# Rounding of the feed-forward rows on GpSimd, tiles written out, the last tile in quarters, and small steps with two tensors

## The reference

```python
x = x + xattn(layernorm(x), ctx)              # 16 heads, 1024 keys per batch
x = x + ffn(layernorm(x))                     # hidden width 2048

def bit_linear(x, w, b):
    gamma_x = clip(max(abs(x), axis=-1), 1e-5)
    x_dq = clip(round(x * 127 / gamma_x), -128, 127) * gamma_x / 127
    gamma_w = clip(mean(abs(w)), 1e-5)
    w_dq = clip(round(w / gamma_w), -1, 1) * gamma_w
    return x_dq @ w_dq.T + b

def ffn(x):
    return bit_linear(silu(bit_linear(x, gate_w, gate_b)) * bit_linear(x, val_w, val_b), out_w, out_b)
```

## Time and profile before

| what | us |
|---|---|
| three runs | 858.44, 861.84, 864.04 |
| median | 861.84 |
| profiled execution, span from first to last instruction (the page gives no other time of it) | 861.5 |
| TensorE busy | 757.3 (88%) |
| VectorE busy | 766.2 (89%) |
| ScalarE busy | 573.6 (67%) |
| GpSimd busy | 577.6 (67%) |

### The profile page before, as it was taken

One profiled execution on the slowest core, in us unless ns is written; L12 is line 12 of the kernel. 1 busy time (PEld: TensorE's weight loads), 2 busy tenths in 40 slices (PEclk: granted clock), 3 DMA queues, 4 the chain that ended last, 5 costly groups with the idle time before them and its releaser, 6 DMA issues.

```text
span 861.5 us, 12578 instructions
## 1 busy us (share of the span) xinstructions
PE 757.3 (88%) x3268; PEld 487.1 (57%) x3268; DVE 766.2 (89%) x1026; ACT 573.6 (67%) x838; POOL 577.6 (67%) x581
## 2 busy tenths in 40 slices
PE   3678998989999999999999999999999675868996
PEld 3555565756666666666566656665666442424543
DVE  5799899989998999899989999999999767797895
ACT  2477677767766867687667766776777576774332
POOL 5769674867486757766776668576848474867462
PEclk9889999999999999999999999999999797889999
DMA  9216867776768576858676766677668999400000
GB/s 330 79 49 115 169 130 140 138 167 134 151 114 170 117 161 132 170 111 167 118 160 134 152 128 138 149 137 150 125 146 213 241 227 275 164 0 25 13 24 37
DMA packets 294405, 118.50 MB, mean 138 GB/s; under 512 B 271856, under 2 KB 278000, under 8 KB 294128
## 3 DMA queue, kind: packets, MB, share of 16 engines
q1 hardware_dynamic: 293568, 116.68, 62.0%
q10 hardware_dynamic: 816, 1.57, 0.5%
HBM read 49.02 MB, written 2.10 MB: 59 GB/s over the span
## 4 chain that ended last, share of the span: by engine, by line
PE 35%; POOL 20%; DVE 18%; issue 11%; DMA 7%; SPq 5%; ACT 3%; POOLq 1%; DVEq 0%; ACTq 0%
PE banks L1419 22%; POOL rot_cos L1055 5%; PE scores L1720 5%; DMA load<-in_pack 4%; POOL rot_lo L1063 4%; SPq L943 4%; PE scores L1507 3%; PE banks L1735 3%; DVE neg_max L1323 3%; POOL rot_hi L1061 2%; DVE rows L1330 2%; POOL rot_sin L1046 2%; DVE rot_cos L1295 2%; DVE cv_lo L1288 1%; POOL wq_lo L388 1%
## 5 line engine op out<-in xcount | busy, mean ns | idle before, releaser
L1185 ACT ACTIVATE scores<-scores,neg_max 128x1024 f32<-128x1024 f32 x128 | 139.2, 1087 | 56.1 <-DVE neg_max L1323 54.6
L1330 DVE SCALAR_TENSOR_TENSOR rows<-scores,rows 128x1024 f16<-128x1024 f32 x128 | 154.9, 1220 | 13.7 <-ACT rows L1196 12.6
L1419 PE MATMUL banks<-pt,v_hi 128*128 128x512 f16 x512 | 154.3, 383 | 12.5 <-DMA pt<-rows 11.4
L1323 DVE TENSOR_REDUCE neg_max<-scores 128x1 f32<-128x1024 f32 x128 | 155.5, 1216 | 2.9 <-PE scores L1507 2.7
L1055 POOL TENSOR_TENSOR rot_cos<-rot_cos,rot_sin 128x512 f32<-128x512 f32 x93 | 119.2, 1281 | 46.6 <-DVE rot_sin L1297 42.2
L1196 ACT ACTIVATE rows<-scores 128x1024 f16<-128x1024 f32 x128 | 130.8, 1022 | 5.2
L1063 POOL TENSOR_TENSOR rot_lo<-rot_cos,rot_hi 128x512 fp32r<-128x512 f32 x93 | 119.6, 1286 | 7.8
L1159 ACT CAST cv_hi<-banks 128x512 fp32r<-128x512 f32 x64 | 37.6, 587 | 102.6 <-PE banks L1419 101.4
L1318 DVE SCALAR_TENSOR_TENSOR acc<-banks,inv,acc 128x512 f32<-128x512 f32 x128 | 91.4, 745 | 8.0 <-PE banks L1419 4.1
L1419 PE MATMUL banks<-pt,v_lo 128*128 128x512 f16 x256 | 97.8, 382 | 0.0
L1419 PEld LDWEIGHTS banks<-pt,v_hi 128*128 128x128 f16 x512 | 44.5, 98 | 79.2 <-issue 36.4
(11 more groups left out here) (211 smaller groups left out, 1824.7 us busy)
## 6 DMA issues: line engine op xcount, KB each, us to landing
load<-in_pack SPq DMA_DIRECT2D x15, 320.0 KB, 3.5
raw_chunk<-in_out_w SPq DMA_DIRECT2D x8, 512.0 KB, 5.2
raw_chunk<-in_gate_w SPq DMA_DIRECT2D x8, 512.0 KB, 4.4
raw_chunk<-in_val_w SPq DMA_DIRECT2D x8, 512.0 KB, 4.6
raw<-in_gate_w SPq DMA_DIRECT2D x8, 512.0 KB, 5.5
raw<-in_val_w SPq DMA_DIRECT2D x8, 512.0 KB, 5.2
raw<-in_out_w SPq DMA_DIRECT2D x8, 512.0 KB, 7.0
load<-in_pack SPq DMA_DIRECT2D x15, 256.0 KB, 3.3
```

The costliest lines, as they stand in the source:

```text
L1185: nc.scalar.activation(scores[:, u % 2, :], scores[:, u % 2, :], ACT.Exp, bias=neg_max[:, u:u + 1], accum_out=sums[:, u:u + 1]).then_inc(e ...
L1323: nc.vector.tensor_reduce(neg_max[:, u:u + 1], scores[:, u % 2, :], AX, ALU.max, negate=True).then_inc(max_ready, 1)
L1330: nc.vector.scalar_tensor_tensor(out=rows[:, u % ROWS, 1, :], in0=scores[:, u % 2, :], scalar=WEIGHT_LIFT, in1=rows[:, u % ROWS, 0, :], op ...
L1419: mm = nc.tensor.matmul(out, ws[a], xs[c], start=first and n == 0, stop=last and n == 2)
```

## The change

Four things, in the order of the code:

- In LAST_DVE `sum` stands first and `G` moves ahead of `low 7 last`.
- In the second norm, var_eps, x_gamma, x_gate and x_val become operations with two tensors: the constants come from a new tile `const`, filled by GpSimd at the start, or from `gamma`, spread over four columns.
- All eight feed-forward tiles are written out. round_down leaves VectorE; GpSimd does it right after the second product of the next tile, for tiles 0 to 6. It waits for the lift and, as h_quant is single, for the turn of the tile before.
- The last tile goes in quarters. Its first three maxima are taken during tile 7, its lift, rounding, turn, copy and contraction go by 512 columns, with banks of their own in `scores` (`ps_last`), another output bank (`ps_x`) and a buffer of its own (`ht_last`, where gate was).

```diff
 LAST_DVE = (
-    ("max", 0), ("low", 7, "last"), ("sum",), ("max", 1), ("low", 0), ("G",), ("low", 1), ("max", 2), ("low", 2), V1,
+    ("sum",), ("max", 0), ("G",), ("low", 7, "last"), ("max", 1), ("low", 0), ("low", 1), ("max", 2), ("low", 2), V1,
...
-        nc.vector.tensor_scalar(self.var_eps[:, half], self.mv[:, half, 1], EPS, None, ALU.add).then_inc(self.var_ready, 1)
+        nc.vector.tensor_tensor(self.var_eps[:, half], self.mv[:, half, 1], self.const[:, 0:1].to_broadcast([P, U]),
+                                ALU.add).then_inc(self.var_ready, 1)
...
-        self.link(dve, nc.vector.tensor_scalar(x_gamma, self.most[:, half], 1e-5, 1.0 / 127.0, ALU.max, ALU.mult))
+        self.link(dve, nc.vector.scalar_tensor_tensor(out=x_gamma, in0=self.most[:, half], scalar=1e-5,
+                                                      in1=self.const[:, 1:2].to_broadcast([P, U]), op0=ALU.max, op1=ALU.mult))
...
-            nc.vector.tensor_scalar(t[name][:, half], x_gamma, t["gamma"][:, w:w + 1], None, ALU.mult)
+            nc.vector.tensor_tensor(t[name][:, half], x_gamma, t["gamma"][:, w:w + 1].to_broadcast([P, U]), ALU.mult)
...
     def run(engine, tile, after):
-        for n in range(U):
+        for n in range(NU):
             tile(Head(n), min(n, 2))
-        with engine.Fori(0, (NU - U) // 2) as i:
-            for odd in range(2):
-                tile(Head(U + odd, i), 2)
         after(Head(NU - 2), Head(NU - 1))
...
         def last_contract(h, k):
-            if k == 0:
-                pe.wait_ge(out_done, h.after(1, 0))
             pe.wait_ge(last_copied, k + 1)
-            for c in range(k * HC // 2, (k + 1) * HC // 2):
-                mm = nc.tensor.matmul(ps_o[:], ht[:, c, :], out_t[:, c, :], start=c == 0, stop=c == HC - 1)
+            for c in range(k * HC // NH, (k + 1) * HC // NH):
+                mm = nc.tensor.matmul(ps_x[:], ht_last[:, c, :], out_t[:, c, :], start=c == 0, stop=c == HC - 1)
...
     def tensor_tokens(pe):
         def after(h6, h7):
             turn(h6)
             contract(h6)
             last_turn(0)
             last_turn(1)
+            last_turn(2)
             last_contract(h7, 0)
+            last_turn(3)
             last_contract(h7, 1)
+            last_contract(h7, 2)
+            last_contract(h7, 3)
...
     def vector_tokens(dve):
         def tile(h, before):
             for n in range(NP):
                 scale(h, n, before)
+                if h.number == NU - 1 and n >= NP - 3:
+                    last_part(h, n - NP + 3)
...
-                if before and n == (6 if before == 1 else 5):
-                    round_down(h.plus(-1))
...
         def after(h6, h7):
             copy_ht(h6)
             last_range(h7)
             last_round(h7, 0)
+            last_round(h7, 1)
+            last_round(h7, 2)
             finish(h6)
             last_copy(h7, 0)
-            last_round(h7, 1)
+            last_round(h7, 3)
             last_copy(h7, 1)
+            last_copy(h7, 2)
+            last_copy(h7, 3)
             finish(h7)
...
     def scalar_tokens(act):
-            for k in range(2):
-                nc.scalar.activation(hidden[:, s, half_of(k)], hidden[:, s, half_of(k)], ACT.Identity, bias=t["magic"][:],
+            for k in range(NH):
+                nc.scalar.activation(hidden[:, s, part_of(k)], hidden[:, s, part_of(k)], ACT.Identity, bias=t["magic"][:],
...
     def gpsimd_tokens(pool):
+        def round_down(h):
+            pool.wait_ge(h_lifted, h.after(1, 1))
+            if h.number or h.i is not None:
+                pool.wait_ge(ht_full, h.after(1, 0))
+            nc.gpsimd.tensor_scalar(h_quant[:], hidden[:, h.number % 2, :], MAGIC + 127, MAGIC, ALU.min,
+                                    ALU.subtract).then_inc(h_rounded, 1)
...
                 nc.gpsimd.tensor_tensor(hidden[:, h.number % 2, part_of(n)], sigma[:, part_of(n)],
                                         val[:, part_of(n)], ALU.mult).then_inc(hidden_ready, 1)
+                if before and n == 1:
+                    round_down(h.plus(-1))
                 if before == 1 and n < 2:
                     raw.clip(pool, LOTS_WITH_HEAD + n)
```

More of the change, by code:

```diff
@@ L704, in spread @@
         nc, half = self.nc, slice(b * U, (b + 1) * U)
+        dve.wait_ge(self.t["constants"], 1)
         dve.wait_ge(self.seen, U * (b + 1))
@@ L1078, in prepare @@
                 nc.gpsimd.memset(t["minus_magic"][:], -MAGIC)
+                nc.gpsimd.memset(second.const[:, 0:1], EPS)
+                nc.gpsimd.memset(second.const[:, 1:2], 1.0 / 127.0)
                 nc.gpsimd.memset(t["ones"][:], 1.0).then_inc(t["constants"], 1)
@@ L1667, in feed_forward @@
     ht = over("ht", [P, HC, P], at["pt_lo"] + 2 * HID, BF16)
+    ps_last = scores[:].rearrange("p u n -> p (u n)").bitcast(BF16).rearrange("p (k n) -> p k n", k=NH)
+    ht_last = over("ht_last", [P, HC, P], at["v_hi"], BF16)
     h_max, h_gamma, h_scale, h_out = (over(n, [P, 2], next(small)) for n in ("h_max", "h_gamma", "h_scale", "h_out"))
@@ L1755, in last_turn @@
             pe.wait_ge(last_rounded, k + 1)
-            for c in range(k * HC // 2, (k + 1) * HC // 2):
-                mm = nc.tensor.transpose(ps_h[:, c * P:(c + 1) * P], h_quant[:, c * P:(c + 1) * P], t["ident_b"][:])
+            for c in range(k * HC // NH, (k + 1) * HC // NH):
+                at = c % (HC // NH) * P
+                mm = nc.tensor.transpose(ps_last[:, k, at:at + P], h_quant[:, c * P:(c + 1) * P], t["ident_b"][:])
             mm.then_inc(last_turned, 1)
         def last_contract(h, k):
-            if k == 0:
-                pe.wait_ge(out_done, h.after(1, 0))
             pe.wait_ge(last_copied, k + 1)
-            for c in range(k * HC // 2, (k + 1) * HC // 2):
-                mm = nc.tensor.matmul(ps_o[:], ht[:, c, :], out_t[:, c, :], start=c == 0, stop=c == HC - 1)
-            if k:
+            for c in range(k * HC // NH, (k + 1) * HC // NH):
+                mm = nc.tensor.matmul(ps_x[:], ht_last[:, c, :], out_t[:, c, :], start=c == 0, stop=c == HC - 1)
+            if k == NH - 1:
                 mm.then_inc(out_full, 1)
@@ L1802, in range_of @@
             nc.vector.reciprocal(h_scale[:, one], h_gamma[:, one]).then_inc(h_range, 1)
[L1804 to L1808, removed]
         def copy_ht(h):
@@ L1820, in finish @@
             tile = acc(h.after(1, 0))
-            nc.vector.scalar_tensor_tensor(out=tile, in0=ps_o[:], scalar=h_out[:, one],
+            src = ps_x if h.number == NU - 1 else ps_o
+            nc.vector.scalar_tensor_tensor(out=tile, in0=src[:], scalar=h_out[:, one],
                                            in1=tile, op0=ALU.mult, op1=ALU.add).then_inc(out_done, 1)
@@ L1846, in tile, with last_part @@
                     second.scales(dve, 1)
+        def last_part(h, n):
+            dve.wait_ge(hidden_ready, h.after(NH, n + 1))
+            nc.vector.tensor_reduce(last_max[:, n:n + 1], hidden[:, h.number % 2, part_of(n)], AX, ALU.max,
+                                    apply_absolute_value=True).then_inc(last_parts, 1)
         def last_range(h):
             one = slice(h.number % 2, h.number % 2 + 1)
-            for n in range(NH):
-                dve.wait_ge(hidden_ready, h.after(NH, n + 1))
-                nc.vector.tensor_reduce(last_max[:, n:n + 1], hidden[:, h.number % 2, part_of(n)], AX, ALU.max,
-                                        apply_absolute_value=True).then_inc(last_parts, 1)
+            last_part(h, NH - 1)
             dve.wait_ge(last_parts, NH)
@@ L1864, in last_round @@
             dve.wait_ge(last_lifted, k + 1)
[L1865 removed]
+            nc.vector.tensor_scalar(h_quant[:, part_of(k)], hidden[:, h.number % 2, part_of(k)], MAGIC + 127, MAGIC, ALU.min,
                                     ALU.subtract).then_inc(last_rounded, 1)
         def last_copy(h, k):
[L1869 to L1870 removed]
             dve.wait_ge(last_turned, k + 1)
[L1872 removed]
+            nc.vector.tensor_scalar(ht_last[:].rearrange("p c s -> p (c s)")[:, part_of(k)], ps_last[:, k, 0:512], -128.0, None,
                                     ALU.max).then_inc(last_copied, 1)
@@ L1936, in tile @@
                 pool.wait_ge(out_bias_loaded, 16)
-            if h.i is not None:
+            if h.number > U:
                 pool.wait_ge(second.normed_ready, NU)
```

7 lines of the change are left out of this document (1 added, 6 removed).

## The result

The changed kernel takes 882.57 us (median; 881.58 to 884.61) beside 861.92 for the kernel before: 1.0246 times as long, interval 1.0215 to 1.0278. Forecast were 856.8 us and a range of 852.5 to 861.0. The change is 20.7 us slower, on the side to which the prediction gave 4 in 100.

What follows compares the result with a forecast made beforehand. TensorE was taken to bound full feed-forward tiles, 11.25 us each, so gains came only where it waits. Tile 1 +1.2, tiles written out -3.8 and tail -2.4 made -5.0: from 861.84 to 856.8 us, range 852.5 to 861.

Steps and rivals of the forecast that it cites:

- the side to which the prediction gave 4 in 100: Whole kernel: measured slower than 870.5 us, chance 0.04, half of the slow-rounding rival's.
- I take 1.9, since the form is the clip's; only the output type differs: GpSimd's rounding over 128x2048: priced at 1.9 us from the weight lot's clip, median 1.894 us.
- The upper bound of 5.1 us: GpSimd's rounding: duration at the rate of the two-tensor products, 1.275 us for 512 columns.
- The fourth rival: GpSimd's rounding takes 5.1 us; tile 1, tail and four full tiles lose time: +7.8 us, 869.6 us; chance 0.08.
- The cover of 1.6 us: Full tiles: GpSimd's fourth product ends 1.6 us before its maximum starts, so rounding under 3.5 us costs 0.
- Tile 1, +1.2: Rounding delays GpSimd's bias addition in tile 1; x_val waits, tile 2's first val and contraction come later: +1.2 us.
- Tiles written out, -3.8: Tile 4 waits for five token rows instead of eight; TensorE's idle and low clock go: -3.8 us.
- the 1.83 of low clock: Tile 4's start: 20 matmuls and a turn took 7.04 us against 5.21 at full rate; 1.83 us taken away.
- Tail, -2.4: Last tile in quarters with earlier maxima: last sum -3.0 us, half of 1.08 low clock given back: -2.4 us.
- the second rival: Tail's gaps bring low clock over tile 6's contraction, 2.6 us more, tail about 0: 859.2 us; chance 0.17.
- Small steps, 0: Second norm: two-tensor steps still wait for GpSimd's running instruction as before; price 0, bounds -1.8 us and 0.
- Up to 680 us the change touches nothing but one order on VectorE: Before the feed-forward stage: only VectorE's order of sum and G changes, priced 0, bounds -0.4 and +0.4.

Runs made afterwards that it cites:

- fast rounding: Changed kernel with GpSimd's rounding as multiply by one and add of the negated constant, clip at 127 left out; 851.15 us, 0.9891 of the kernel before.
- two fast instructions: Changed kernel with GpSimd's rounding as two instructions, min and max in place, then multiply and add to bf16; 859.31 us, 0.9982 of the kernel before.
- fast rounding, wait back: Changed kernel with rounding as multiply and add, tiles 4 to 7 again waiting for all eight token rows before their first projection; 851.17 us.
- rounding on VectorE: Changed kernel with only the rounding of tiles 0 to 6 back in its old place on VectorE; 853.86 us, 0.9923 of the kernel before.
- both runs of forms: Changed kernel with a different form of GpSimd's rounding instruction in each of tiles 0 to 6, seven forms per run; instructions took 1.9, 5.4 or 7.1 us.

## Why the prediction was wrong, step by step

The starts of the final sums, read from the timelines, in us after the first gate of tile 0, show where each part lies. Each set of figures comes from one profile. The first profile of before is that of the prediction.

| kernel | to sum of tile 1 | tile 1 to 2 | tile 2 to 5 | tile 5 to 7 | all |
|---|---|---|---|---|---|
| before, first and second profile | 48.17, 46.94 | 16.09, 14.42 | 33.75, 33.75 | 17.55, 17.56 | 115.56, 112.67 |
| before, written out | 47.99 | 12.13 | 33.76 | 16.46 | 110.34 |
| changed | 53.71 | 17.02 | 47.36 | 21.67 | 139.76 |
| fast rounding | 46.64 | 12.27 | 33.76 | 16.35 | 109.02 |
| two fast instructions | 49.37 | 12.32 | 35.50 | 18.91 | 116.10 |
| fast rounding, wait back | 46.61 | 12.63 | 33.76 | 16.35 | 109.35 |
| fast rounding, tail in halves | 45.65 | 12.28 | 33.76 | 16.24 | 107.93 |
| fast rounding, small steps back | 47.90 | 12.13 | 33.76 | 14.74 | 108.53 |
| fast rounding, old order of sum and G | 46.60 | 12.27 | 33.76 | 16.35 | 108.98 |
| rounding on VectorE | 46.97 | 12.13 | 33.75 | 19.33 | 112.18 |

**The step that failed: "I take 1.9, since the form is the clip's; only the output type differs".** The output type was innocent; the operations differed, and that was not counted as a difference. Every tensor-scalar of GpSimd in the kernel before is (mult, add) or (min, max), the fast pairs, so that no row could show what another pair costs. The upper bound of 5.1 us was too low as well. The fourth rival had the mechanism, but at 0.08 its chance was set by the size and form of the nearest row alone. By its own working a rounding of 7.08 gives -5.0 + 2 x 5.2 + 4 x 3.6 = +19.8; measured is +20.7. That it meets so well is partly luck: the slow form costs 31 us over the fast one, not 2 x 5.2 + 4 x 3.6 = 24.8, and the rest gains 9 to 10, not 5. By the table a full tile loses 4.5 to 4.8 us instead of 3.6: 0.2 more because the round leaves less room than the cover, and 0.8 because the other steps of the round grow from 8.0 to 8.8 us, with TensorE at a lower granted clock.

The Trainium skill, GPSIMD Engine Reference, section Engine selection, calls a one-input operation on GpSimd roughly line-rate, and gives two-input ones as about twice as slow as on VectorE. Here the one-input pair (min, subtract) takes 7.08 us on GpSimd and 1.22 on VectorE; for (min, max) and (mult, add), at 1.9, the sentence fits better.

**The cover of 1.6 us, "decides from 3.5 us on, at about 3.8 the whole gain is gone":** nearly right. The round of waits gives 3.3, and with 3.8 us the ratio is 0.998, though 8.2 us of a gain of 9.4 went, where the prediction had 5 of 5. The way to it was incomplete: the prediction looked at GpSimd's own queue and not at the loop from the rounding through turn, copy, maximum and lift back to the next rounding.

**Tile 1, +1.2:** not seen with the two-tensor steps. x_val slipped in ahead of the bias addition (0.15 us at 763.60 in the fast version), the lower bound. To the sum of tile 1 the fast version takes 46.64 us, before 46.94 to 48.17. But with the small steps undone the term is there. The fast version, then the one with tensor-scalar steps:

```profile
763.60 0.15 DVE L750 TENSOR_TENSOR x_val<-x_gamma,gamma 128x4 f32<-128x4 f32 x1
```

```profile
766.87 1.31 DVE L748 TENSOR_SCALAR x_val<-x_gamma,gamma 128x4 f32<-128x4 f32 x1
```

The bias addition starts 0.01 us after x_val in the first and 0.02 in the second, where x_val ends with it. The first val of tile 2 comes 1.1 us later for it, the contraction behind starts after an idle of 2.25 us instead of 1.11 and takes 5.31 us at a granted clock of 0.68 instead of 3.63 at 1.00, and the sum of tile 1 comes at 47.90 instead of 46.64. x_val takes 0.15 in every profile with a fast rounding and two-tensor steps, and 1.31 in the one with tensor-scalar steps. So the edit of the small steps may be what kept this term at 0; whether it was the form or the hundredths between the two starts was not tried.

**Tiles written out, -3.8:** right in mechanism, and in size within the interval of the part alone, -2.6 to -6.5 us (tile 1 to 2: 12.13 against 16.09 and 14.42). Of the two terms, the idle of 1.99 us is in both profiles of before; the 1.83 of low clock is only in the first, where the turn behind it took 1.91 us instead of 1.06. But it isn't the wait alone that makes the stall. In the fast version token row 7, the last, is taken 49.6 us after the first gate, instead of 52.7 and 51.4, so it is in time and the wait finds it there. The trace offers a reason: before, ScalarE's take of that row stands behind a sigma for which it sits idle 2.39 us, until VectorE, with its rounding of 1.22 us just done, has scaled the gate; in the fast version, with the rounding gone from VectorE, that idle is 0.42 us. No run puts the wait back with the rounding on VectorE, so this part is argued and not shown.

**Tail, -2.4:** the second rival held. The third maximum delays the copy, TensorE's gap grows to 2.19 us (2.1 was forecast), and tile 6's contraction takes 5.31 us at a granted clock of 0.68 instead of 3.63 at 1.00; in the version with the rounding on VectorE it takes 6.39 at 0.56. Where the clock stays up, in the version with the small steps undone, the stretch is 14.74 against 17.55, so -2.8, near the bound of -3.0. But 1.3 of that is the clock of the old tail, whose last contraction ran at 0.80 there: halves at the full clock take 16.24, and beside them the quarters gain 1.5. The gap ahead of tile 6's contraction was 2.41 us where the clock stayed up, so the gap's length alone doesn't say which way it falls; that stays open.

**Small steps, 0:** right in time, as far as the runs can tell, and right that two-tensor steps wait; what the price left out may be the 1.2 us of tile 1 above. The profile with the steps undone lost it there and had the high clock in the tail to make up for it. In the changed kernel a two-tensor step still ends with GpSimd's instruction:

```profile
728.81 1.98 POOL L1635 TENSOR_SCALAR raw<-raw,inv_gamma 128x2048 f32<-128x2048 f32 x1
728.86 0.14 DVE L750 TENSOR_TENSOR x_gate<-x_gamma,gamma 128x4 f32<-128x4 f32 x1
728.93 1.87 DVE L750 TENSOR_TENSOR x_val<-x_gamma,gamma 128x4 f32<-128x4 f32 x1
```

**"Up to 680 us the change touches nothing but one order on VectorE":** wrong by an allocation. -3.8 us came from the 8 bytes of const. With that, the parts priced by the prediction come to 0.9891 / 0.9956 = 0.9935, -5.6 us, known to some 4 us either way, beside the sum of -5.0. So for a rounding of 1.9 us the sum's total held, but not term by term: +1.2 for tile 1 did not come and most of -2.4 for the tail did not either, and that these two cancel is luck.

## What to carry to other kernels

- A price read off a neighbouring row holds for the same operations, not for the same shape: where the pair of operations has no row of its own, it can be several times slower, and a run of forms, one per tile, settles it at once. Here multiply by one and add in place of min and subtract turned +2.5% into -1.1%.
- When an instruction goes to another engine, follow the whole round from it back to itself, with every engine on the way; the slack is what the round leaves of the tile's pitch (11.25 - 7.95 = 3.3 us here, an estimate), not the cover in one queue.
- A new small tile moves all that is allocated behind it; profile again with the old offset before a gain or loss is put down to the code.

## What the runs showed of the hardware

GpSimd's time for a 128x2048 tensor-scalar goes by the operations: 1.9 us for (mult, add), (add, mult), (min, max) and a copy, 5.4 for one operation alone, 7.1 for the other pairs tried. One operation is thus slower than two.

The slow form doesn't hold VectorE up. In the changed kernel the second half's steps run inside a rounding, and so they do in both runs of forms (x_gamma 0.15 us beside a rounding of 7.10 and one of 5.37):

```profile
758.73 7.08 POOL L1944 TENSOR_SCALAR h_quant<-hidden 128x2048 bf16<-128x2048 f32 x1
...
763.63 0.15 DVE L746 SCALAR_TENSOR_TENSOR x_gamma<-most_second,const_second 128x4 f32<-128x4 f32 x1
763.82 0.18 DVE L748 RECIPROCAL x_scale_second<-x_gamma 128x4 f32<-128x4 f32 x1
763.91 0.13 DVE L750 TENSOR_TENSOR x_gate<-x_gamma,gamma 128x4 f32<-128x4 f32 x1
763.96 0.15 DVE L750 TENSOR_TENSOR x_val<-x_gamma,gamma 128x4 f32<-128x4 f32 x1
```

By the rule of the Trainium skill, SBUF — State Buffer, section Who interferes with whom, beside which the price of the small steps was set, x_gamma would wait here until 765.81, 2.2 us. It takes 0.15. Behind the fast lift the rule holds for x_val (1.87), though x_gate, 0.05 us after the lift's start, took 0.14.

The transposing transfers land in 3.8 us where the tiles start at a multiple of 64 bytes (one offset) and in 4.4 to 4.5 where they start 32 bytes off it (two offsets), some 3 us over fourteen heads. The Trainium skill, DMA: Bandwidth & Descriptors, section DMA Transpose (X-bar), asks for 32 bytes; all three offsets meet that, and they differ in time all the same.
